# Weights' transposes and gram products in turns of four heads, the first tokens' moments between copies, and the first weights in two transfers

## What is computed

```python
q = rms_norm(x @ q_w + q_b, nq_s).reshape(B, S, H, D)              # H = 16, D = 128, q_w (256, 2048)
k_img = rms_norm(img_ctx @ ki_w + ki_b, nki_s).reshape(B, -1, H, D)
v_img = (img_ctx @ vi_w + vi_b).reshape(B, -1, H, D)
out_img = sdpa(q, k_img, v_img)
...
x = x + jnp.tanh(g_xattn[0]) * _L0_xattn_ref(_layernorm(x, axis=-1), ctx_2048, ...)
```

## Time and profile before

| | us |
|---|---|
| median of 3 runs | 1356.98 |
| lowest, highest | 1355.42, 1357.06 |
| the profiled execution | 1356.92 |
| its span, first to last instruction | 1355.1 |

### The profile page before, as it was taken

One profiled execution on the slowest core, in us unless ns is written; L12 is line 12 of the kernel. 1 busy time (PEld: TensorE's weight loads), 2 busy tenths in 40 slices (PEclk: granted clock), 3 DMA queues, 4 the chain that ended last, 5 costly groups with the idle time before them and its releaser, 6 DMA issues.

```text
span 1355.1 us, 26606 instructions
## 1 busy us (share of the span) xinstructions
PE 1326.7 (98%) x10367; PEld 1155.5 (85%) x10367; DVE 767.6 (57%) x2315; ACT 765.8 (57%) x2092; POOL 74.1 (5%) x114
## 2 busy tenths in 40 slices
PE   7899999999999999999999999999999999999998
PEld 6788888988898788988889888998889888888777
DVE  7644555546555464665555465564656555554575
ACT  4375666566465574756556565556646556466522
POOL 3000000010000000000000100001000000001010
PEclk9999999999999999999999999999999999999999
DMA  8312522224122321222212231122312112122100
GB/s 303 110 63 79 141 94 68 75 63 125 48 70 64 102 94 47 63 94 79 94 47 71 70 125 63 47 79 82 110 44 79 63 63 94 48 78 65 62 1 32
DMA packets 51451, 108.47 MB, mean 80 GB/s; under 512 B 8224, under 2 KB 32000, under 8 KB 50688
## 3 DMA queue, kind: packets, MB, share of 16 engines
q1 hardware_dynamic: 51328, 106.77, 24.3%
HBM read 89.98 MB, written 16.78 MB: 79 GB/s over the span
## 4 chain that ended last, share of the span: by engine, by line
PE 86%; DVE 10%; ACT 3%; issue 1%; DMA 0%; SPq 0%; DVEq 0%
PE bank L114 57%; PE bank L1053 8%; PE bank L1063 5%; PE bank L1024 3%; PE bank L1042 3%; PE bank L1163 2%; PE bank L1175 2%; PE bank L1205 1%; PE bank L1014 1%; PE bank L1117 1%; ACT xn L785 1%; PE bank L994 1%; DVE rstd L80 1%; DVE logit L1534 1%; DVE ao_lo L1525 1%
## 5 line engine op out<-in xcount | busy, mean ns | idle before, releaser
L114 PE MATMUL bank<-sv,ct_hi 128*128 128x256 f32 x1024 | 195.7, 289 | 0.0
L114 PE MATMUL bank<-so,ao_hi 128*128 128x256 f32 x1016 | 188.2, 284 | 0.3 <-DVE ao_lo L1525 0.3
L1525 DVE SCALAR_TENSOR_TENSOR ao_lo<-bank,vecs,ao_hi 128x512 fp32r<-128x512 f32 x127 | 95.3, 751 | 159.7 <-ACT ao_hi L754 158.9
L760 ACT ACTIVATE expo<-logit,least 128x64 f32<-128x64 f32 x512 | 171.6, 337 | 20.6 <-DVE least L1536 20.6
L754 ACT ACTIVATE ao_hi<-bank,vecs 128x512 fp32r<-128x512 f32 x127 | 87.0, 685 | 155.0 <-PE bank L1053 154.5
L114 PEld LDWEIGHTS bank<-so,ao_hi 128*128 128x128 f32 x1016 | 162.4, 189 | 8.5 <-issue 0.5
L114 PEld LDWEIGHTS bank<-sv,ct_hi 128*128 128x128 f32 x1024 | 156.6, 189 | 0.1
L1534 DVE TENSOR_TENSOR logit<-bank,rr 128x256 f32<-128x256 f32 x128 | 54.4, 425 | 162.4 <-PE bank L1063 161.9
L779 ACT ACTIVATE q_sb<-bank,qbias,qscale 128x512 f32<-128x512 f32 x128 | 99.3, 776 | 80.3 <-PE bank L114 79.8
L114 PE MATMUL bank<-sv,ct_lo 128*128 128x256 f32 x512 | 143.1, 279 | 0.0
L114 PE MATMUL bank<-so,ao_lo 128*128 128x256 f32 x508 | 142.3, 280 | 0.0
(11 more groups left out here) (239 smaller groups left out, 2668.0 us busy)
## 6 DMA issues: line engine op xcount, KB each, us to landing
sv<-v_scratch SPq DMA_DIRECT2D x56, 512.0 KB, 3.4
so<-o_scratch SPq DMA_DIRECT2D x56, 512.0 KB, 3.3
xin<-in_x_dram SPq DMA_DIRECT2D x8, 512.0 KB, 4.8
cin<-in_ctx_dram SPq DMA_DIRECT2D x32, 128.0 KB, 4.8
xres<-in_x_dram SPq DMA_DIRECT2D x8, 512.0 KB, 4.7
c_scratch<-cs SPq DMA_DIRECT2D x8, 512.0 KB, 5.0
v_scratch<-sv SPq DMA_DIRECT2D x8, 512.0 KB, 3.1
o_scratch<-so SPq DMA_DIRECT2D x8, 512.0 KB, 2.6
```

The costliest lines, as they stand in the source:

```text
L114: last = pe.matmul(out, lhs[a], rhs[b], start=start and n == 0, stop=stop and n == 2, **kw)
L760: last = act.activation(expo[:, t, :], logit[:, t, :], ACT.Exp, scale=-1.0, bias=least[:, t:t + 1], accum_out=rsum[:, t:t + 1])
L1525: dve.scalar_tensor_tensor(out=lo[:, :], in0=attention_bank(g, h)[:, :], scalar=vecs[:, v:v + 1], in1=hi[:, :].bitcast(F32), op0=ALU.add, ...
```

## The change

- **Loads.** The left quarter of both row parts of q_w is loaded first, in two transfers on one signal; the rest of both comes behind the vectors.
- **PE.** The transposes and the gram products of a weight go in turns of four heads: turn f of both row parts (two banks), then the gram products of those four heads, accumulated in two banks of their own (4 and 5). The turns use four banks in rotation. The order is turn 0, turn 1, gram 0, turn 2, gram 1, turn 3, gram 2, gram 3. The first tokens' transposes are split in two pairs, one in front of the first two turns of ki_w and one behind them; before, all four stood behind all of ki_w's transposes.
- **DVE.** Copies follow the turns. The moments' statistics stand before the last two copies of q_w, variances and scales behind them, and `low_part(0)` behind the scales, no longer ahead of the statistics. `low_part(3)` stands between the second and third turn's copies of ki_w, and the splits before the fourth.
- **ACT.** `high_part(2)` goes ahead of `normalise(0)`; two of the four token copies go ahead of `high_part(3)`.
- **The first projection** waits for one copy fewer (its bank isn't the gram's).

```diff
-PREP_BANKS = 6
+TURN_BANKS = 4
...
-        sp.dma_start(raw[0][:, 0:INNER // 2], q_w[0:P, 0:INNER // 2]).then_inc(s_first, 16)
+        for c in range(DC):
+            sp.dma_start(raw[c][:, 0:INNER // 4], q_w[c * P:(c + 1) * P, 0:INNER // 4]).then_inc(s_first, 16)
         for j, v in enumerate((q_b, nq_s, nki_s, ki_b, vi_b)):
             sp.dma_start(vrow[j * H:(j + 1) * H, :], v.rearrange("(h d) -> h d", h=H)).then_inc(s_vec, 16)
-        sp.dma_start(raw[0][:, INNER // 2:], q_w[0:P, INNER // 2:]).then_inc(s_raw[0], 16)
-        sp.dma_start(raw[1][:, :], q_w[P:2 * P, :]).then_inc(s_raw[1], 16)
+        for c in range(DC):
+            sp.dma_start(raw[c][:, INNER // 4:], q_w[c * P:(c + 1) * P, INNER // 4:]).then_inc(s_raw[c], 16)
...
         high_part(0)
         high_part(1)
+        high_part(2)
         normalise(0)
-        high_part(2)
+        transposed(0, 0)
+        transposed(0, 1)
         high_part(3)
-        for t in range(NT):
-            transposed(0, t)
+        transposed(0, 2)
+        transposed(0, 3)
...
+        def turn_weight(n, f):
+
             for c in range(DC):
+                i, j = 2 * n + c, 2 * f + c
+                if f == 0 and n == 0:
+                    pe.wait_ge(s_first, 32)
+                elif f <= 1:
                     pe.wait_ge(s_raw[i], 16)
+                if j >= TURN_BANKS:
+                    pe.wait_ge(s_prepev, 2 + 10 * n + j - TURN_BANKS + 1)
+                elif n == 1:
+                    pe.wait_ge(s_prepev, 2 + j + TURN_BANKS + 1)
+                b = banks[j % TURN_BANKS]
+                for k in range(4):
+                    h = 4 * f + k
+                    last = pe.transpose(b[:, k * P:(k + 1) * P], raw[i][:, h * P:(h + 1) * P], ident[:, :])
+                last.then_inc(s_prep, 1)
+
+        def gram_matrix(n, f):
+
+            pe.wait_ge(s_prepev, 2 + 10 * n + 2 * f + 2)
+            for c in range(DC):
+                for h in range(4 * f, 4 * f + 4):
+                    last = pe.matmul(banks[TURN_BANKS + c][:, c * P:D + 1], wt[:, h, c * P:(c + 1) * P],
+                                     wt[:, h, c * P:D + 1], start=h == 0, stop=h == H - 1)
+                if f == 3:
                     last.then_inc(s_prep, 1)
...
-        turn_weight(0)
-        gram_matrix(0)
-        turn_weight(1)
-        for t in range(NT):
-            transposes(-1, t)
-        gram_matrix(1)
+        turn_weight(0, 0)
+        turn_weight(0, 1)
+        gram_matrix(0, 0)
+        turn_weight(0, 2)
+        gram_matrix(0, 1)
+        turn_weight(0, 3)
+        gram_matrix(0, 2)
+        gram_matrix(0, 3)
+        transposes(-1, 0)
+        transposes(-1, 1)
+        turn_weight(1, 0)
+        turn_weight(1, 1)
+        transposes(-1, 2)
+        transposes(-1, 3)
+        gram_matrix(1, 0)
+        turn_weight(1, 2)
+        gram_matrix(1, 1)
+        turn_weight(1, 3)
+        gram_matrix(1, 2)
+        gram_matrix(1, 3)
         pe.wait_ge(s_wlo["dve"], len(DVE_LOWS))
         pe.wait_ge(s_wlo["pool"], len(POOL_LOWS))
-        pe.wait_ge(s_prepev, PREP_USES - 1)
+        pe.wait_ge(s_prepev, PREP_USES - 2)
         project(0, 0, 0)
...
-        weight_copies(0)
-        low_part(0)
+        bias_column(0)
+        for f in range(3):
+            weight_copies(f)
         tile_stats(0)
+        weight_copies(3)
         tile_variances()
         tile_scales()
+        low_part(0)
         gram_copies(0)
+        bias_column(1)
+        weight_copies(0)
         weight_copies(1)
         low_part(3)
+        weight_copies(2)
         split(0, 0)
         split(0, 1)
+        weight_copies(3)
         gram_copies(1)
```

More of the change, by code:

```diff
@@ L706, in high_part @@
             if i == 0:
-                act.wait_ge(s_first, 16)
+                act.wait_ge(s_first, 32)
             act.wait_ge(s_raw[i], 16)
@@ L964, in _ @@
     def _(pe):
[L965 to L973, removed]
+        def turn_weight(n, f):
             for c in range(DC):
-                i = 2 * n + c
-                if i > 0:
+                i, j = 2 * n + c, 2 * f + c
+                if f == 0 and n == 0:
+                    pe.wait_ge(s_first, 32)
+                elif f <= 1:
@@ L977, in turn_weight @@
                     pe.wait_ge(s_raw[i], 16)
[L978 to L986, removed]
-                    last.then_inc(s_prep, 1)
@@ L1375, in _ @@
         pe.wait_ge(s_vec, 80)
-        pe.transpose(prep_bank()[:, 0:5 * H], vrow[:, :], ident[0:5 * H, 0:5 * H]).then_inc(s_prep, 1)
+        pe.transpose(banks[TURN_BANKS][:, 0:5 * H], vrow[:, :], ident[0:5 * H, 0:5 * H]).then_inc(s_prep, 1)
         pe.wait_ge(s_ones, 1)
         pe.wait_ge(s_chain, BSQ_READY)
-        pe.matmul(prep_bank()[:, 0:2 * H], ones[:, :], bsq[:, :, :].rearrange("p n h -> p (n h)"),
+        pe.matmul(banks[TURN_BANKS + 1][:, 0:2 * H], ones[:, :], bsq[:, :, :].rearrange("p n h -> p (n h)"),
                   start=True, stop=True).then_inc(s_prep, 1)
-        turn_weight(0)
-        gram_matrix(0)
-        turn_weight(1)
-        for t in range(NT):
-            transposes(-1, t)
-        gram_matrix(1)
+        turn_weight(0, 0)
[18 more added lines that the diff above has]
+        gram_matrix(1, 3)
         pe.wait_ge(s_wlo["dve"], len(DVE_LOWS))
         pe.wait_ge(s_wlo["pool"], len(POOL_LOWS))
-        pe.wait_ge(s_prepev, PREP_USES - 1)
+        pe.wait_ge(s_prepev, PREP_USES - 2)
         project(0, 0, 0)
@@ L1421, in _, with prepared, bias_column, weight_copies @@
         use = [0]
-        def prepared():
+        def prepared(bank):
             use[0] += 1
             dve.wait_ge(s_prep, use[0])
-            return banks[(use[0] - 1) % PREP_BANKS]
-        def weight_copies(n):
+            return banks[bank]
+        def bias_column(n):
             v = (0, 3)[n] * H
             dve.tensor_copy(wt[:, :, D:D + 1], vecs[:, v:v + H].unsqueeze(2))
+        def weight_copies(f):
             for c in range(DC):
-                for f in range(4):
-                    dve.tensor_copy(wt[:, 4 * f:4 * f + 4, c * P:(c + 1) * P],
-                                    prepared()[:, :].rearrange("p (h n) -> p h n", h=4)).then_inc(s_prepev, 1)
+                b = prepared((2 * f + c) % TURN_BANKS)
+                dve.tensor_copy(wt[:, 4 * f:4 * f + 4, c * P:(c + 1) * P],
+                                b[:, :].rearrange("p (h n) -> p h n", h=4)).then_inc(s_prepev, 1)
         def low_part(i):
@@ L1452, in gram_copies @@
         def gram_copies(n):
-            b = prepared()
+            b = prepared(TURN_BANKS)
             dve.tensor_copy(gram[:, n, 0, 0:P], b[:, 0:P])
             dve.tensor_scalar(gram[:, n, 0, P:D + 1], b[:, P:D + 1], 2.0, None, ALU.mult).then_inc(s_prepev, 1)
-            b = prepared()
+            b = prepared(TURN_BANKS + 1)
             dve.tensor_copy(gram[:, n, 1, P:D], b[:, P:D])
@@ L1849, in end @@
             residual(LAST, "y", 1, y_full, tg[:, 3:4], x, y_ready)
-        dve.tensor_copy(vecs[:, :], prepared()[:, 0:5 * H]).then_inc(s_prepev, 1)
+        dve.tensor_copy(vecs[:, :], prepared(TURN_BANKS)[:, 0:5 * H]).then_inc(s_prepev, 1)
         dve.wait_ge(s_prepev, 1)
@@ L1857, in _ @@
         chain.mark(dve.tensor_tensor(qbias[:, :], vecs[:, 0:H], qscale[:, :], ALU.mult))
-        dve.tensor_reduce(beta[:, :], prepared()[:, 0:2 * H].rearrange("p (n h) -> p n h", n=2), AXX,
+        dve.tensor_reduce(beta[:, :], prepared(TURN_BANKS + 1)[:, 0:2 * H].rearrange("p (n h) -> p n h", n=2), AXX,
                           ALU.add).then_inc(s_prepev, 1)
-        weight_copies(0)
-        low_part(0)
+        bias_column(0)
+        for f in range(3):
+            weight_copies(f)
         tile_stats(0)
+        weight_copies(3)
         tile_variances()
         tile_scales()
+        low_part(0)
         gram_copies(0)
+        bias_column(1)
+        weight_copies(0)
         weight_copies(1)
         low_part(3)
+        weight_copies(2)
         split(0, 0)
         split(0, 1)
+        weight_copies(3)
         gram_copies(1)
```

## The result

The changed kernel takes 1361.86 us (median of 6 runs, 1360.37 to 1362.51) against 1356.26 (6 runs, 1355.33 to 1357.20) of the kernel before: 5.6 us or 0.4% slower, ratio 1.0038 with a 95% interval of 1.0027 to 1.0050. The forecast was 1361.0, with 1355.7 to 1362.6 as its range. The profiled execution took 1362.29 us, its span is 1360.5; before they were 1356.92 and 1355.1.

The account below looks back on a forecast made before the run. PE, busy 98% of the span, was taken as the bound, read at the first projection's start. A 2.4 us later projection plus 1.7 for the clock gave 4.1 on 1356.92: 1361.0, range 1355.7 to 1362.6.

Parts of the forecast that it names:

- First instruction held: In the first tokens' moments, DVE's first Newton multiply at 20.2 us would stand until POOL's k_lo ends at 23.6.
- ki_w's landing: The first half of ki_w would land at 17.2 us instead of 16.7, so POOL starts k_lo at 19.1.
- the shift of 0.47: One more load issue on SP's queue was taken to move every landing behind it by 0.47 us.
- The clock: After PE's stand ahead of the tokens' transposes, half clock for 3.4 us would lose 1.7 us (ends 0 and 3.4).
- Rival 3: DVE's hold begins ahead of the Newton steps, or PE's half clock lasts twice as long: +5.5 us, 1362.4; chance 0.06.
- The later falls: PE's half clock from 61.7 and from 167.5 us in the kernel before; the forecast's sum had no term for them.
- rival 4: PE dense up to the first projection at 39.3, one later clock fall gone: -2.0 - 1.7 us, 1353.2; chance 0.05.
- The q stage: PE's q transposes and first gram: first quarter starts at about 10.9 us, the end comes at 23.3 against 24.44.
- the 4.4 of the sum: PE would stand 4.4 us, from the first gram's end at 23.3 until the tokens are ready at 27.7.
- DVE and ACT behind it: DVE's low parts and gram copies and ACT's fourth rounding stay hidden under PE's work, low_part(3) with over 2 us to spare.
- Rival 2: DVE isn't held by POOL: tokens ready at 24.3, first projection at 40.3, -1.0 us, 1355.9; chance 0.17.
- Rival 1: PE stands 4.4 us ahead of the tokens' transposes, but the clock stays full: +2.4 us, 1359.3; chance 0.22.

Follow-up runs that it names:

- z1_after: The changed kernel once more, unaltered, on the chip of three other follow-up runs: 1361.46 us, ratio 1.0034.
- x3_awake: The changed kernel with four matmuls of no use in PE's stand ahead of the first tokens' transposes: 1360.08 us, ratio 1.0026.
- x4_loads: The changed kernel with the loads of the kernel before and the waits that go with them: 1359.44 us, ratio 1.0019.
- x1_pool_late: The changed kernel with one wait more: POOL begins k_lo only after DVE has copied the q gram: 1356.87 us, ratio 1.0003.
- y1_act_alone: The kernel before with only ACT's third rounding moved ahead of the normalisation of the first tokens: 1357.60 us, ratio 1.0008.
- z3_moments_alone: The kernel before with only the moments moved: statistics ahead of the last two q copies, low_part(0) behind the scales: 1359.10 us, ratio 1.0018.
- y4_all: The kernel before with gram quarters, token pairs, matmuls of no use in the 3.02 us stand and sixteen at PE's start: 1352.62 us, ratio 0.9976.

## Why the prediction was right, and where not

**Right as a whole, and in its mechanism.** ACT's moved rounding, POOL's earlier start, the hold of DVE's small instructions, the stand of PE ahead of the tokens' transposes and the fall of the clock are all in the trace, and the runs that remove one of them remove its cost. That the total came out 0.9 us from the forecast is in part luck: two terms were too small by 2.7 us together, and a later clock fall, which the sum left out of account, was missing for 1.4.

**First instruction held.** The forecast took the first product of two SBUF operands, the Newton multiply, and named the tensor_scalar in front of it as the Trainium skill's case (SBUF — State Buffer, § Who interferes with whom). The trace agrees with the page: `var_eps` itself stood 3.01 us. From the end of the hold to ACT's start it took 27.30 - 24.90 = 2.4 us instead of 1.97, so 0.4 us were missing.

**ki_w's landing.** Mis-sized by 1.1 us: 18.3 (8.52 + 9.8) instead of 17.2. The step that failed is the shift of 0.47 taken for everything behind. SP issued the context's four pieces in 3.10 us where it took 2.67 before, so ki_w was issued 0.9 later, and took 0.7 longer to land. The 0.9 recurs: in all six traces with the new loads ki_w was issued at 8.3 to 8.6, in the eight with the old ones at 7.6 to 7.8. The landing scatters: in `z1_after` k_lo started at 19.51, only 0.4 behind the forecast's 19.1. In the first trace the tokens were ready at 29.4, not 27.7: 1.25 us from POOL's later start and 0.4 from the line above.

**The clock.** Mis-sized by 1.0: 18.66 us from the tokens' transposes to the projection, against 16.0, is 2.7 where 1.7 was taken. (At the full clock this work takes 15.7 by `x3_awake`, so the clock itself cost 3.0, and the 16.0 held 0.3 too many.) The low window was 6.8 us long, not 3.4, and 6.0 of it fell on work. Rival 3 had this as its condition. The 1.7 that the forecast took from the earlier trace rows isn't the price of every fall. It held in `x4_loads`, whose low window was 3.5 us long.

**The later falls.** The sum had no term for them; only rival 4 let one go. The stand of 3.02 us is still there in the changed kernel, before 67.54, but brought no fall in either of its traces; why is open. That it went was worth -1.4 and covered half of what the two terms above lacked: 4.1 + 1.7 + 1.0 - 1.4 = 5.4, the difference of the profiled executions.

**The q stage.** The forecast had its end at 23.3. The first trace shows 25.95: PE waited for q_w's second rest (landed near 11.1 instead of 10.4), the four transposes behind it took 0.91 us where the forecast had some 0.45, and the first gram quarter, from 12.10 and not 10.9, went at half pace until about 15. `z1_after` shows 23.8. Either way it was hidden, as forecast: the stand was 3.5 us in the one and 4.8 in the other, around the 4.4 of the sum.

**DVE and ACT behind it** stayed hidden: PE has no wait between 29.43 and 48.09.

**The rivals.** Rival 2 (DVE isn't held) is out as a fact, but `x1_pool_late` is what it describes, and its projection at 42.8 shows that its sum of 40.3 was too low: the first Newton multiply comes at 22.99 and not at 20.2, because the last copies of q_w, which stand ahead of it, wait for the slower q stage. Rival 1 (clock stays) is `x3_awake`: 44.7 at the projection, 43.7 by the rival's sum. Rival 3, given 0.06, had the two things that the traces show in place of the forecast's: the hold began ahead of the Newton steps (0.4 of its 1.05 us), and the low clock, fallen while PE stood, lasted twice as long. The projection came 6.8 us later, more than rival 3's 5.5; it is the missing later fall that brings the whole back to the forecast.

## What to carry to other kernels

An engine off the path can still hold another: here a POOL subtraction of 4.5 us held a DVE instruction over 4 numbers for up to 4.3. Before an instruction of ACT or POOL is moved forward because its input is there, look which small DVE steps will now run beside POOL's long one, and who waits for them. A stand of PE can cost more than its length: here 3 us more through the clock. Work put ahead of a late input (here k's transposes ahead of the tokens') hides both. Changes under 0.3% are read best at a fixed point of the trace, with the clock falls counted apart.

## What the hardware showed that I had not expected

- A DVE tensor_scalar of 4 numbers and a copy of 16, both inside SBUF, beside a POOL subtraction end only with it (3.01, 4.30 and 1.90 us instead of 0.17), while batch statistics, their aggregation and copies out of PSUM are not.
- Low stretches come in two lengths: 6.8 and 6.9 us in the two traces of the changed kernel, against 3.4 and 3.5 for those in the earlier trace rows and 3.5 in `x4_loads`. That the clock falls while PE stands doesn't make the difference: in `y1_act_alone` it fell at 61.2, 0.4 us before the stand's end, and the stretch was 3.5 us. In the changed kernel it fell 0.8 and 1.1 us before the end. What sets the length is open. PE's timeline of `y1_act_alone`, then the window:

```profile
61.61 0.80 PE L114 MATMUL bank<-ct_hi,k_hi 128*128 128x512 f32 x1 [3.03 <-ACT v_sb L776]
```

```profile
61.20:64.70 3.50, 3.09 (x10) 2.06 (x12) 2.01 (x10) 1.66 (x4) 0.00 (x0) 0.51 0.42 170
```

- The same stand of 3.02 us doesn't always bring a fall: it did in 7 of the 12 traces in which it wasn't filled, and the later stand of 1.62 us did in 12 of 14. In `z3_moments_alone` the first one stands there as before, and the windows behind it stay at 1.00; what tells the traces apart is open. PE's timeline of `z3_moments_alone`, then its window over 58 to 70 us:

```profile
62.77 0.50 PE L114 MATMUL bank<-ct_hi,k_hi 128*128 128x512 f32 x1 [3.02 <-ACT v_sb L776]
```

```profile
58.00:70.00 12.00, 8.97 (x64) 7.29 (x64) 7.23 (x25) 7.56 (x24) 0.69 (x1) 1.00 0.33 131
```

- At the start PE's transposes and gram records go at half pace with the granted clock column at 1.00 (and 12 to 15 us of the changed kernel). In `y4_all`, where the sixteen matmuls of no use stand before them, 11 transposes start at 8 to 9 us, with the DMA engines busy for 0.99 of the time, against 7 and 0.97 at 9 to 10 us in the kernel before. So the slow pace belongs to PE's start and not to the loads, and the column doesn't show it.
